# One block for sorting and planning the edges of a four-layer graph network, with the second edge order built beside the first units

## The reference

```
L0: agg = segment_sum(h[src], type34 * n + dst); mean = agg / max(cnt, 1)        # 34 * 625 segments
    h1  = einsum('rni,rio->no', mean, W_rel) + h @ W_root + b;  then one GCN layer
L1: two GCN layers (sum over edges with 1/sqrt(deg) on both ends, times W)
L2: h = [h, node_emb[node_type]] (896 wide); three RGCN layers:
    xw = h @ w_rel[r] per relation (3); msg = xw[type3, src] / count[dst, type3]; sum at dst; + h @ w_root + b; relu
L3: one GCN layer
```

## Time and profile before

| | us |
|---|---|
| median of the runs (3) | 1888.14 |
| the profiled execution | 1889.03 |
| its span, first to last instruction | 1887.3 |
| TensorE busy | 1670.8 (89%) |
| VectorE busy | 1138.9 (60%) |
| block 1, sort, root product | 0 to 119.5 |
| block 2, plan | 119.5 to 225.0 |
| block 3, units | 225.0 to 963 |
| block 4, layers | 963 to 1887.3 |

### The profile page before, as it was taken

The page is one execution under the profiler, slowest core; times in us unless marked ns, Lnnn a source line. Parts: engine busy times, 40 slices in busy tenths (PEclk is TensorE's granted clock), DMA queues, the critical chain, the costliest instruction groups (busy, mean ns, idle before and its releaser), DMA issues. The chain is left out here.

```text
span 1887.3 us, 29761 instructions
## 1 busy us (share of the span) xinstructions
PE 1670.8 (89%) x10079; PEld 1550.1 (82%) x10080; DVE 1138.9 (60%) x1877; ACT 617.4 (33%) x832; POOL 367.6 (19%) x298
## 2 busy tenths in 40 slices
PE   2756439999999999999948997999989999899988
PEld 1653438989898989999838996999979999899988
DVE  7979787767777668766446464533544345445463
ACT  3000025656565555655331223212222122222220
POOL 5120115555554344333200000000000000000000
PEclk9877569999999999999969998999989999999999
DMA  5000138889888779978551123202212122222011
GB/s 158 22 22 1 47 126 234 254 225 263 250 231 231 217 206 246 259 202 255 127 118 39 53 65 85 84 13 75 72 46 63 42 75 67 67 67 66 27 53 45
DMA packets 94146, 226.43 MB, mean 120 GB/s; under 512 B 10344, under 2 KB 33882, under 8 KB 94090
## 3 DMA queue, kind: packets, MB, share of 16 engines
q1 hardware_dynamic: 71231, 153.30, 25.9%
q0 software_dynamic: 19104, 70.00, 16.1%
q10 hardware_dynamic: 3755, 2.36, 0.5%
HBM read 186.27 MB, written 39.36 MB: 120 GB/s over the span
## 5 line engine op out<-in xcount | busy, mean ns | idle before, releaser
L930 PE MATMUL layers_ps_o<-layers_w_hi,layers_g_hi 128*125 128x384 f32 (+1 forms) x1040 | 362.7, 349 | 4.4 <-DVE layers_w_lo L794 3.2
L931 PE MATMUL layers_ps_o<-layers_w_lo,layers_g_hi 128*125 128x384 f32 (+1 forms) x1040 | 361.2, 347 | 0.0
L932 PE MATMUL layers_ps_o<-layers_w_hi,layers_g_lo 128*125 128x384 f32 (+1 forms) x1040 | 360.8, 347 | 0.0
L1944 PE MATMUL l_means_ps<-l_means_w_hi,l_means_g_hi 128*128 128x512 f32 (+1 forms) x912 | 237.5, 342 | 0.0
L1944 PE MATMUL l_means_ps<-l_means_w_hi,l_means_g_lo 128*128 128x512 f32 (+1 forms) x912 | 235.6, 340 | 0.0
L1944 PE MATMUL l_means_ps<-l_means_w_lo,l_means_g_hi 128*128 128x512 f32 (+1 forms) x912 | 234.7, 339 | 0.0
L1610 ACT CAST l_means_w_hi<-l_means_w_raw 128x768 fp32r<-128x768 f32 x204 | 170.3, 838 | 185.2 <-PE l_means_ps L1944 185.0
L958 PE MATMUL layers_ps_g<-a,h_hi 125*128 125x316 f32 x840 | 196.8, 316 | 33.9 <-DVE h_lo L416 16.9
L1793 DVE TENSOR_TENSOR l_means_w_lo<-l_means_w_raw,l_means_w_hi 128x768 fp32r<-128x768 f32 x204 | 186.4, 946 | 62.2 <-ACT l_means_w_hi L1610 62.2
L930 PEld LDWEIGHTS layers_ps_o<-layers_w_hi,layers_g_hi 128*125 128x125 f32 x1040 | 194.4, 187 | 14.2 <-issue 4.3
L932 PEld LDWEIGHTS layers_ps_o<-layers_w_hi,layers_g_lo 128*125 128x125 f32 x1040 | 194.2, 187 | 5.4
(11 more groups left out here) (323 smaller groups left out, 2378.2 us busy)
## 6 DMA issues: line engine op xcount, KB each, us to landing
l_means_w_raw<-in_L_gnn_W_rel SPq DMA_DIRECT2D x204, 384.0 KB, 6.5
layers_w_raw<-in_L_gnn_w_rel SPq DMA_DIRECT2D x39, 384.0 KB, 3.5
layers_w_raw<-in_L_gnn_w_rel SPq DMA_DIRECT2D x21, 448.0 KB, 3.9
layers_a_raw<-adj SPq DMA_DIRECT2D x9, 769.0 KB
layers_w_raw<-in_L_gnn_W SPq DMA_DIRECT2D x18, 384.0 KB, 5.1
l_means_list_now<-targets SPq DMA_DIRECT2D x34, 192.0 KB
layers_w_raw<-in_L_gnn_w_root SPq DMA_DIRECT2D x13, 384.0 KB, 3.7
layers_w_raw<-in_L_gnn_w_root SPq DMA_DIRECT2D x7, 448.0 KB, 4.2
```

What stands on the lines that cost most here:

```text
L930: t.matmul(out, g_hi[:, f, rows], w_hi[:, f, cols], start=(f == 0), stop=False)
L931: t.matmul(out, g_hi[:, f, rows], w_lo[:, f, cols], start=False, stop=False)
L932: mm = t.matmul(out, g_lo[:, f, rows], w_hi[:, f, cols], start=False, stop=(f == fc - 1))
L1944: mm = t.matmul(ps_y[j][:, o0:o1], g[:, f, at], w[:, f, o0:o1], start=(f == 0 and opens and g is g_hi and w is w_hi), stop=(f == fc - 1 an ...
```

## The change

`sort_edges`, `normalise_rows`, `root_rows` and `plan_units` are replaced by one function `prepare`. The places of the edges come from three sets of TensorE products into six PSUM banks: earlier partitions of the same key, earlier columns, and the base of the key. Keys, slots and tiles are f16 throughout, and the iotas they are compared with are copied out by ScalarE instead of written by GpSimd. Nodes of a unit are counted from one-hots of 31 tiles at a time, over the slots. Ranks of nodes come from products with a lower triangle. The root product is in plain f32, in ten halves, with no split operands. The same block gathers the first unit's rows and loads its weights. Its one-hots of tile have the 17 columns innermost. In outline:

```diff
-def sort_edges(...)      -def normalise_rows(...)      -def root_rows(...)      -def plan_units(...)
+def prepare(nc, tag, types, units, src, dst, etype, x_dram, w_root, bias, w_first, x, h, ident, slot_dst, src_index,
+            row_index, row_inv, plan, dinv, rows, sums, spare_rows, targets, e_raw, w_raw):
+    chunk = 17; group = tiles // 6; per = BANK // EC; rank_banks = -(-types // per)      # 17, 31, 6, 6
+  SyncE: src, dst; x in 10 DMAs; bias, w_root; spare rows; after normal: rows; w_first; sums of tiles 0..3 as they are
+         taken; after list_copied: targets; after the last o_taken: sums of tile 4; waits for all of them
+  GpSimd: small constants; after sources_ready and rows_stored: indirect DMA of e_raw for the first unit
+  ScalarE: DMA of etype; key_iota, earlier_keys, diagonal_keys (34 * 85 each), slot_iota (128 * 17), tile_iota (186 * 17);
+         sqrt; relu of the rows with scale and shift (5 x 768); copies of turned rows; node_iota (125 * 31); take(0..9)
+  VectorE:
+            v.tensor_tensor(is_key, key_iota, key[:].unsqueeze(1).broadcast_to([EP, types, EC]), ALU.is_equal)
+            v.tensor_tensor(offsets, earlier_keys, tile_sums[:].unsqueeze(1).broadcast_to([EC, EC, types]), ALU.mult)
+            v.tensor_scalar(bases, diagonal_keys, base[:, 0:1], float(lot_slots), ALU.mult, ALU.mult)
+            for b0, b1 in ((0, 3), (3, rank_banks - 1), (rank_banks - 1, rank_banks)):
+                then(v.tensor_tensor(banked(place[:, k0 * EC:k1 * EC]), ps_rank[:, b0:b1, 0:cols], ..., ALU.mult))
+            while left > 1: ...                                  # six halvings of the 34 planes
+            def slots_of_chunk(n):                               # n = 0..4
+                if n >= 2: dve.wait_ge(chunk_used, n - 1)
+                then(v.tensor_tensor(is_slot[:], slot_iota[:], slot_of..., ALU.is_equal))               # 128 * 17
+                v.tensor_tensor(is_tile[:, n % 2], tile_iota[:], tile_of..., ALU.is_equal)              # 186 * 17
+                for i in range(2): v.tensor_tensor(at_slot[:, n % 2, i], is_slot[:], loads..., ALU.mult)
+            slots_of_chunk(0); plan entries; row statistics; slots_of_chunk(1..4)
+            for n in range(tiles // group):                      # 6
+                v.tensor_tensor(is_node[:, n % 2], node_iota, node_of..., ALU.is_equal)                 # 125 * 31
+            def is_rank_of(i):                                   # i = 0..9
+                v.tensor_tensor(is_rank[:, i % 2], rank_iotas, rank_lo..., ALU.is_equal)                # 128 * 31
+  TensorE: tile sums (34), three sets of ranks (6 each, up to 510 columns);
+            slots(0)
+            for f in range(fc): turn(f)
+            slots(1); root(0); slots(2); root(1); root(2); slots(3); root(3); slots(4)
+            counts(0); counts(1); root(4); counts(2..5); node ranks; turned counts; root(5); whole counts; root(6)
+            for i in range(2 * NT):
+                invert(i)
+                if i == 4: root(7)
+            ...                                                  # two transposes of the lists
+            root(8); root(9)
+            # root(n): 1 + 6 matmuls of 384 columns, f32;  slots(n): 34 of 186 columns, is_tile[:, n % 2, :, c]
+            # counts(n): 31 of 5 columns;  invert(i): 31 of 9 columns
```

In `add_means` the first gather and weights are gone, and the second order of edges moves:

```diff
-COLUMNS = 5
+COLUMNS = 17
+LEAD = 4
-            gather(0, 1)
+            nc.gpsimd.nop().then_inc(index_ready, 1)
-            iota(slot_iota[:], [[1, SLOT], [0, COLUMNS]])
-            iota(tile_iota[:], [[1, tiles2]])
-            iota(node_iotas[:], [[1, NP], [0, LOTS]])
-            positions()
-            embeddings()
             make_pick(0)
             ...
+            for n, beside in enumerate((keys_of_edges, running_counts, places_by_key, places)):
+                one_unit(n, beside)                              # places also runs embeddings()
+            dve.wait_ge(iotas_ready, 3)
             with dve.Fori(0, list_units) as n:
-                one_unit(unit(n), lambda: columns(n))
+                one_unit(unit(n + LEAD), lambda: columns(n))
             def columns(n, ...):                                 # is_slot: 128 * 17; is_tile planes: 120 * 17 each
-                for c in range(COLUMNS):
-                    for i in range(2):
-                        ins = v.tensor_scalar(is_tile[:, c, i, :], tile_iota[:], hi[:, col], loads[:, i, col], ...)
+                v.tensor_tensor(is_tile[:, 0], tile_iota[:], tile_of..., ALU.is_equal)
+                v.tensor_tensor(is_tile[:, 1], is_tile[:, 0], values[:, 1, at]..., ALU.mult)
+                v.tensor_tensor(is_tile[:, 0], is_tile[:, 0], values[:, 0, at]..., ALU.mult)
-                    mm = t.matmul(ps_b[:, 0:2 * tiles2], is_slot[:, :, c], is_tile[:, c, :, :].rearrange(...), ...)
+                    mm = t.matmul(ps_b[:, 0:2 * tiles2], is_slot[:, :, c], is_tile[:, :, :, c], ...)
+            # TensorE: Fori(0, 2) units, the two count matmuls, Fori(2, LEAD), Fori(0, list_units) with columns, ...
+            # ScalarE, after its unit 3: copies slot_iota (128 * 17), tile_iota (120 * 17), node_iotas (125 * 4)
```

In `layer` the scaling moves from the chunks to `take`, and only the first RGCN layer counts:

```diff
-                v.tensor_scalar(inv[:], ps_g[:, 0, LEFT:LEFT + NC], 1.0, None, ALU.max).then_inc(g_freed, 1)
-                v.reciprocal(inv[:], inv[:]).then_inc(inv_ready, 1)
-                        v.tensor_tensor(scaled[:, f % 2, :], ps_g[:, (f + 1) % 2, LEFT:LEFT + NC], inv[:], ALU.mult)
+                if count_rows:
+                    v.tensor_scalar(tmp[:], ps_g[0:NP, 1, 0:2 * NT]..., 1.0, None, ALU.max)
+                    v.reciprocal(rstd[:], tmp[:]); v.tensor_scalar(here, rstd[:], 1.0, None, ALU.mult)
+                for f in range(fc):
+                    w_low(s, f)
+                    g_low(s, f, ps_g[:, f % 2, LEFT:LEFT + NC])
+                take(s, False, last, r)                          # scale = inv_rows[:, r * NT + d]
-                for k in range(NT):
-                    for p in range(2):
-                        mm = t.matmul(ps_g[:, 0, at:at + PART[p]], ones[:], a[:, k, cols], ...)
+                if count_rows:
+                    for d in range(NT):
+                        for k in range(NT):
+                            mm = t.matmul(ps_g[0:NP, 1, 2 * d:2 * d + 2], a[:, k, column(d):column(d) + NP], ones[:], ...)
+        rgcn(1, wide, wide, keep_rows=True, count_rows=True)
```

More of the change, by code:

```diff
@@ L800, in g_low, with take @@
                             ALU.subtract).then_inc(g_ready, 1)
-        def take(s, first, last):
+        def take(s, first, last, relation=None):
             for d in range(NT):
@@ new lines, in _ @@
+            take(1)
+            s.copy(rank_iotas[:, mid:SLOT, :],
+                   rank_iota[0:NP, mid:SLOT].unsqueeze(2).broadcast_to([NP, mid, part_units])).then_inc(rank_iota_ready, 1)
+            take(2)
+            for k in range(NT):
+                s.copy(third_iota[:, k], iota[0:NP, 0:UNIT].unsqueeze(2).broadcast_to([NP, UNIT, units]))
+            s.copy(node_number[:], node_col[:].unsqueeze(2).broadcast_to([NP, NT, units])).then_inc(rank_iota_ready, 1)
+            take(3)
+            take(4)
@@ new lines, in slots @@
+            def slots(n):
+                pe.wait_ge(chunk_ready, n + 1)
+                for c in range(chunk):
+                    for i in range(2):
+                        mm = t.matmul(ps_slot[:, i, 0:tiles], at_slot[:, n % 2, i, :, c], is_tile[:, n % 2, :, c],
+                                      start=(n == 0 and c == 0 and i == 0),
+                                      stop=(n == EC // chunk - 1 and c == chunk - 1), skip_group_check=True)
+                mm.then_inc(chunk_used, 1)
@@ new lines, in _ @@
+            pe.wait_ge(consts_ready, 10)
+            pe.wait_ge(keys_ready, 1)
+            for k in range(types):
+                mm = t.matmul(ps_tile[:, k, :], is_key[:, k, :], ones[0:EP, 0:2], start=True, stop=True, skip_group_check=True)
+            mm.then_inc(tiles_summed, 1)
+            for b in range(rank_banks):
+                t.matmul(ranks(b), lower[:], early[0:EP, keys_of(b).start * EC:keys_of(b).stop * EC],
+                         start=True, stop=False, skip_group_check=True)
@@ new lines, in _ @@
+            t.matmul(ps_type_col, behind[:], ones[0:types, 0:2], start=True, stop=True, skip_group_check=True)\
+                .then_inc(types_summed, 1)
+            slots(0)
+            for f in range(fc):
+                turn(f)
+            slots(1)
+            root(0)
+            slots(2)
+            root(1)
+            root(2)
+            slots(3)
+            root(3)
+            slots(4)
+            counts(0)
+            counts(1)
+            root(4)
+            for n in range(2, tiles // group):
+                counts(n)
```

1283 lines of the change are left out of this document (640 added, 643 removed).

## The result

| | us |
|---|---|
| before, median of 4 runs | 1889.05 |
| changed, median of 4 runs (1914.25 to 1917.58) | 1915.8 |
| ratio, 95% interval | 1.0141, 1.0126 to 1.0156 |
| forecast | 1797, 1778 to 1824 |

The change makes the kernel 1.4% slower; the forecast was 92 us faster. In the profiled executions the spans are 1912.6 and 1887.3, a difference of 25.3 us, and this is where it arises. A part starts where its first DMA, table load or product stands in the timeline; the units end where the layers load their rows.

A forecast was written before the change was run, and what follows sets the result against it. VectorE's chain was taken to bound the first 266.6 us, TensorE the units and layers. Terms -57 - 35 + 8 + 3 - 10 = -91 took 1889.03 to 1798.0, median 1797; range 1778 to 1824.

The forecast's parts named there:

- rival 1: Slot and column products: strided moving operand runs at half rate, +21 us, median 1818; chance 0.17.
- the block: Single block replacing the first two: ends at 168 us in place of 225.0, -57; bounds 158 and 185.
- list units: Units with column products: VectorE needs 5.2 us where 6 are free, so no added cost; same 85 products on TensorE.
- 186 small products (12 to 19): Counting nodes by unit in the block: TensorE's products take 12 to 19 us beside 13.4 of one-hots on VectorE.
- Root halves: Ten parts of the float32 root product in the block: 4.5 or 9 us each by clock, all ten 45 or 90.
- Rival 2: Block stays a chain: root halves at 1.2 GHz, two more hand-overs, last three to four +4.5 each, +17: 1814; chance 0.15.
- Rival 4: Slower: broadcast compares at one element a cycle, VectorE paces the block, TensorE stays at 1.2 GHz, 1897 to 1922; chance 0.04.
- chunk 0: First slot chunk on VectorE in the block: 5.9 us after places at 25, ready at 31.
- Start of the units: From block end to the units' first product: 41.6 us before, only list, pick and `e_lo` stay, 6.9; -35.
- lead units: First units, with keys, scan, places and embeddings moved beside them on VectorE: TensorE loses some 8 us, bounds 3 and 32.
- Rival 5: Positions beside the units stall TensorE by all 32 us of them, +24: 1821; chance 0.08.
- Layers: Ones products -13.4, scaling -3.2, small products +8.3, chunk taking -1.8: sum -10 us, bounds -13 and -3.

The follow-up runs named there:

- the run with all three mended: Changed kernel with tile one-hots contiguous by column in slot products and in the units' columns, node one-hots 128 wide: 1825.24 us, ratio to before 0.9662.
- the run in the new order: The run with all three mended, with the fourth and fifth root halves put behind the last slot group: 1815.04 us.
- the positions run: The run with all three mended, but VectorE does keys, counts, places and embeddings before the first unit, as in the kernel before: 1849.64 us.
- the run with the columns contiguous: Changed kernel with only the tile one-hots in add_means (columns of the units and last pass) stored contiguous: 1893.43 us.
- alone -10.5: Kernel before with only the new layers (counts once, in rows, scaling when sums are taken): 1878.39 us, ratio 0.9941.

## Why the prediction was wrong

**The step that failed** is the price of a product in the new block. 0.087 us for 186 columns and 0.0625 us for a small product were read off products whose moving operand was contiguous or whose stationary operand had 128 columns. They were used for slot products and columns whose moving operand has a step of 34 bytes (0.343 us measured for 186 columns), and for counts whose stationary operand has 125 columns at a step of 62 bytes (0.217 us).

- *Slot products.* The forecast named the difference and put half the rate on it as rival 1, +21 us, chance 0.17, because one strided operand, the stationary one of the earlier trace rows, ran at full rate. Mechanism right, size wrong: a quarter of the rate, 43 us more busy time in the block and 28 in the list units (37.8 us for 85 products, 9.8 in the run with all three mended). The stretch from the last unit's last product to the loads of the layers is 4.4 us longer, with VectorE's part. That "the strided weights, read from the same memory, cost nothing" was no evidence: that operand has 128 columns, and the counts show what a large step costs at 125.
- *Counts.* "186 small products (12 to 19)" took 40.4, at 0.217 us each in place of 0.0625. Neither a bound nor a rival held this; 128 columns gave 26.6 us back.
- *Root halves.* 5.0 us at 2.4 GHz (forecast 4.5), 8.6 at the low clock (9). The forecast held the low clock to the last halves; it came to seven of the ten, 71.9 us in all. Rival 2 was this, with 17 us. With all three mended the clock is still 0.67 from 84 to 173 us and the block ends 12 late: 3 of it stand at the end of the slot groups (85.0 us, not 82) and 2 in the last store (6.7 us, not 5). That the other 7 are the clock is argued from the rows, not tested; the run in the new order, 10.2 us quicker, changed the clock and a wait at once.
- *VectorE's prices* came out in the layout of the change: 1.90 us for 3162 elements (1.85), 2.24 (2.2), 2.29 (2.3); chunk 0 ready at 35.3 (31) with places at about 28.6 (25). Rival 4 is out.

```profile
L1064 DVE TENSOR_TENSOR prep_early<-prep_early,prep_rank_lo 125x3968 f16<-125x3968 f16 x10 | 22.5, 2289 | 11.1 <-PE prep_ps L1179 11.1
L1043 DVE TENSOR_TENSOR prep_at_slot<-prep_early,prep_node_of 128x3875 f16<-128x3875 f16 x6 | 13.4, 2244 | 26.0 <-PE prep_ps L1170 25.9
```

- The idle time at the end of these lines is VectorE waiting for TensorE. The forecast made a slow VectorE the way to "slower", decided by a block end past 259; the block ended at 248 and the kernel was slower all the same, since the units lost time too.
- *Start of the units* 8.0 (6.9), *lead units*: waits of 7.1 + 0.7 (8). Right. Rival 5 is out by the positions run.
- *List units.* "Nothing" was wrong twice: 28 us of products, and, once these are mended, more VectorE work than the room of 6 us carries. Of the 46.2 us in the units, 28 + 4.4 + 7.8 are named; about 6 stay. TensorE's granted clock was 0.86 from 325 to 350 and 0.87 to 375, and 0.86 from 400 to 450, where the kernel before had 1.00. In the run with the columns contiguous it was 1.00 from 400 to 450, so the slow products went with the low clock there; from 325 to 350, where TensorE had waited for `g_lo` in a lead unit, it stayed at 0.84. How much of the 6 us is the clock was not measured.
- *Layers* -10.0 (-10), alone -10.5. The 25 small products took 2.63 us a relation (2.8):

```profile
1232.31 2.63 PE layers_ps_g L572 x25
```

- *Range.* It reached only 1824 on the slow side because the price for which there was no row was taken at no more than double. The dearest price of a column in the rows is four cycles, for float32. Taken as a bound over 170 products of 186 columns and 85 of 240, that is 38 + 25 us more at 2.4 GHz and 90 + 60 at 1.2 GHz: an upper end between 1860 and 1947, and the sign open. I had that row and used it for other terms only.

## What to carry to other kernels

Take a product's price from a row with the same step and width in both operands; where there is none, one small run with the layout is worth more than any bound. A layout that suits the writer can cost the reader more: 3162 elements took VectorE 1.90 us with the 17 columns innermost and 3.45 us contiguous (1.5 us a group), but TensorE 11.7 us in place of 2.9 to read them. Look who reads an operand, and how often. When one engine's work shrinks, price the other one's again: here TensorE's busy time rose, and no wait in the trace points to it. What shows it is the time of one product beside the same product elsewhere, and the row of the weight loads beside that of the products.

## What the runs showed of the hardware

- A half-precision moving operand of 186 columns cost 1.84 ns a column at steps of 16 and of 34 bytes (at 34, the same at a granted clock of 1.00 and of 0.50); 0.94 ns at 8 bytes, 0.51 at 4, 0.46 contiguous, these three at 1.00 (2.4 GHz).
- A small product whose stationary operand has a step of 62 bytes took 0.065 us with 128 columns, 0.217 with 125. Contiguous with 125 it took 0.112 us at a clock of 0.50 and 0.060 at 1.00. The profile calls TensorE busy in all of them.
- TensorE, busy for 10.00 of 10 us from 80 to 90, had a granted clock of 0.50, with the end of a slot group (to 83.1) and a root half; in the next 10 us, with root halves at work, it was 0.98. Full busy time is no sign of the high clock.
- VectorE's writes at a step of 34 bytes took 0.43 us for 186 half-precision elements, contiguous 0.18.
